# A feature-interaction tower on one core: the first level of a partial sum goes to an accumulating DMA, and a fourth product chunk is split

## The reference, cut to what matters

```python
e = stack([tbl_f[ids[:, f]] for f in range(39)])      # 1024 samples, 39 fields, 16 values each
x0 = xk = e
for W in (f0, f1, f2):                                # (39*39,128), (128*39,128), (128*39,128)
    z = einsum('bfd,bgd->bfgd', x0, xk).reshape(b, 39 * g, 16)
    xk = einsum('bpd,pm->bmd', z, W)
    outs.append(xk)
z = sum(concatenate(outs, axis=1), axis=-1)           # 1024 x 384
h = relu(concat(z, dense_ctx) @ W_top1 + b_top1)
h = relu(h @ W_top2 + b_top2)
y = h @ W_top3
```

## Time and profile before

| | |
|---|---|
| median of 3 runs (range) | 1400.6 us (1400.31 to 1401.37) |
| the profiled execution, and its span | 1401.89 us, 1400.1 us |
| PE busy | 1297.8 us (93%) |
| POOL busy, without the gaps between the gathers | 1040.9 us (74%) |
| DVE busy | 981.8 us (70%) |
| ACT busy | 773.4 us (55%) |
| mean granted PE clock | 0.999 of full |

### The profile page before, as it was taken

One profiled execution on the slowest core, in us unless ns is written; L12 is line 12 of the kernel. 1 busy time (PEld: TensorE's weight loads), 2 busy tenths in 40 slices (PEclk: granted clock), 3 DMA queues, 4 the chain that ended last, 5 costly groups with the idle time before them and its releaser, 6 DMA issues.

```text
span 1400.1 us, 25243 instructions
## 1 busy us (share of the span) xinstructions
PE 1297.8 (93%) x5629; PEld 982.7 (70%) x5629; DVE 981.8 (70%) x3243; ACT 773.4 (55%) x2449; POOL 1040.9 (74%) x921
## 2 busy tenths in 40 slices
PE   0199999999999999999999999999999999999999
PEld 0167677876787777777777777777778777777754
DVE  2078778586877878587876878688786878688720
ACT  2146666356646665467655566466664576456631
POOL 7668888686887878788886888788786866566530
PEclk9999999999999999999999999999999999999999
DMA  8122121110211121011211112111211101111000
GB/s 218 36 82 55 47 59 53 37 43 24 59 54 51 46 59 53 5 53 46 60 53 51 46 33 58 28 53 46 60 52 52 46 12 55 45 51 45 1 1 0
DMA packets 72379, 67.51 MB, mean 48 GB/s; under 512 B 32140, under 2 KB 44402, under 8 KB 72260
## 3 DMA queue, kind: packets, MB, share of 16 engines
q1 hardware_dynamic: 59556, 62.38, 15.0%
q0 software_dynamic: 9984, 2.58, 1.9%
q10 hardware_dynamic: 2720, 1.48, 0.4%
HBM read 10.15 MB, written 0.00 MB: 7 GB/s over the span
## 4 chain that ended last, share of the span: by engine, by line
PE 65%; DVE 15%; issue 10%; POOL 5%; ACT 2%; DMA 1%; DVEq 1%; SPq 0%; ACTq 0%; POOLq 0%
PE ps L456 13%; PE ps L460 13%; PE ps L457 13%; PE ps L435 13%; DVE terms L809 10%; PE ps L480 5%; DVE prods L781 4%; POOL x_in L328 3%; PE ps L470 3%; PE ps L545 2%; ACT terms L664 2%; PE ps L404 2%; POOL terms L351 2%; PE ps L555 1%; DVEq L808 1%
## 5 line engine op out<-in xcount | busy, mean ns | idle before, releaser
L809 DVE SCALAR_TENSOR_TENSOR terms<-ps,x_scal,terms 128x128 f32<-128x128 f32 x2944 | 814.8, 344 | 294.2 <-PE ps L460 182.6
L664 ACT ACTIVATE terms<-ps,x_scal 128x128 f32<-128x128 f32 x2048 | 586.1, 375 | 388.9 <-PE ps L460 359.8
L351 POOL TENSOR_TENSOR terms<-terms 128x1024 f32<-128x1024 f32 (+2 forms) x384 | 565.6, 1473 | 173.7 <-DVE terms L809 152.9
L456 PE MATMUL ps<-w_high,x_high 128*128 128x512 f32 (+1 forms) x1280 | 581.6, 454 | 3.8 <-ACT terms L664 1.7
L460 PE MATMUL ps<-w_high,x_low 128*128 128x512 f32 (+1 forms) x1280 | 498.7, 390 | 1.1 <-ACT x_rows L607 1.1
L457 PE MATMUL ps<-w_low,x_high 128*128 128x512 f32 (+1 forms) x1280 | 498.3, 389 | 0.0
L328 POOL DMA_INDIRECT x_in<-in_tbl,ids_now x312 | 299.8, 961 | 97.7 <-issue 86.1
L456 PEld LDWEIGHTS ps<-w_high,x_high 128*128 128x128 f32 x1280 | 240.9, 188 | 97.1 <-DVE terms L809 21.7
L457 PEld LDWEIGHTS ps<-w_low,x_high 128*128 128x128 f32 x1280 | 241.6, 189 | 73.5 <-issue 29.8
L460 PEld LDWEIGHTS ps<-w_high,x_low 128*128 128x128 f32 x1280 | 240.9, 188 | 54.5 <-ACT x_rows L607 2.0
L435 PE MATMUL ps<-prods,w 117*128 117x512 f32 x262 | 135.3, 602 | 5.0 <-DVE prods L781 5.0
(11 more groups left out here) (49 smaller groups left out, 525.7 us busy)
## 6 DMA issues: line engine op xcount, KB each, us to landing
prods<-x_cols SPq DMA_DIRECT2D x192, 234.0 KB
x_first<-x_cols SPq DMA_DIRECT2D x96, 78.0 KB
x_in<-in_tbl,ids_now POOLq DMA_INDIRECT x312
x_diag<-x_scal SPq DMA_DIRECT2D x256, 9.8 KB
s<-in_f SPq DMA_DIRECT2D x3, 832.0 KB, 13.3
wt<-in_W_top ACTq DMA_DIRECT2D x1, 768.0 KB, 8.1
wt<-in_W_top ACTq DMA_DIRECT2D x1, 512.0 KB, 9.3
terms<-in_w_pair SPq DMA_DIRECT2D x1, 409.5 KB
```

The source lines that it names most:

```text
L351: nc.gpsimd.tensor_tensor(t[:, 0:n], t[:, 0:n], t[:, n:2 * n], ALU.add).then_inc(s_tree, 1)
L456: nc.tensor.matmul(y, x1_high[:, par, at:at + P], high, start=True, stop=False)
L664: op = nc.scalar.activation(terms[:, u % 2, FB * ACT_BANKS.index(q) + i, :], ps[:, (BANKS * u + q) % RING, i * G:(i + 1) * G], ACT.Copy, s ...
L809: nc.vector.scalar_tensor_tensor(out=acc, in0=y, scalar=x0, in1=acc, op0=ALU.mult, op1=ALU.add).then_inc(s_mac, 1)
```

## The change

1. The tree's widest level goes. In its place POOL adds one pair of slots (128x128), then issues a DMA from its own queue which adds the seven upper slots onto the seven lower ones inside SBUF (128 rows of 896 values, 448 KB). A renumbering of the slots (`SLOTS`) puts DVE's two chains at slots 7 and 15, so that those are the pair that POOL adds itself; ACT's 14 others are the DMA's. POOL then waits for both and goes on with the levels of 4 and 2.
2. The step's two or three gathers are issued between that DMA and the wait for it, and no longer after the step's sum.
3. A fourth chunk of products, number 3, is split as the three others are: one more rounded copy at ACT, one more subtraction at POOL, three passes at PE for one float32 product.
4. PE takes the chunks in the order 4, 5, 6, 0, 1, 2, 3.

```diff
-SPLIT = (0, 1, 2)
+SPLIT = (0, 1, 2, 3)
-CIN1_ORDER = (0, 1, 3, 4, 5, 6, 2)
+CIN1_ORDER = (4, 5, 6, 0, 1, 2, 3)
-HIGHS = ((0, 2), (0, 4), (0, 7))
-POOL_LOWS = {0: (0, 1), 1: (2,)}
+HIGHS = ((0, 2), (0, 4), (0, 7), (0, 9))
+POOL_LOWS = {0: (0, 1), 1: (2, 3)}
-TREE = (8, 4, 2)
+TREE = (4, 2)
+HALF = TERMS // 2
+SLOTS = (HALF - 1, TERMS - 1) + tuple(i for i in range(TERMS) if i % HALF != HALF - 1)
...
                 pool.wait_ge(s_ya, bt * (STEPS * NA) + NA * (u + 1) + CREDIT_A)
                 pool.wait_ge(s_mac, bt * (STEPS * MACS) + MACS * (u + 1) + CREDIT_MAC)
+                nc.gpsimd.tensor_tensor(t[:, HALF - 1], t[:, HALF - 1], t[:, TERMS - 1], ALU.add).then_inc(s_pair, 1)
+                pool.dma_start(out=t[:, 0:HALF - 1], in_=t[:, HALF:TERMS - 1], accum_op=ALU.add).then_inc(s_acc, 16)
+                for f in fetch:
+                    gather(f)
+                pool.wait_ge(s_pair, bt * STEPS + u + 1)
+                pool.wait_ge(s_acc, bt * (16 * STEPS) + 16 * (u + 1))
                 for i, n in enumerate(TREE):
...
-                add_up(bt, wanted)
-                for n in range(STEPS - 1):
-                    for f in share(0, n, STEPS - 1):
-                        gather(f)
-                    add_up(bt, wanted + 1 + n)
+                for n in range(STEPS):
+                    add_up(bt, wanted + n, fetch=share(0, n, STEPS - 1) if n < STEPS - 1 else ())
...
-                        terms[:, u % 2, FB * ACT_BANKS.index(q) + i, :],
+                        terms[:, u % 2, SLOTS[FB * ACT_BANKS.index(q) + i], :],
...
-                    acc = terms[:, u % 2, n % CHAINS, :]
+                    acc = terms[:, u % 2, SLOTS[n % CHAINS], :]
```

More of the change, by code:

```diff
@@ L189, in cin_tower @@
         s_tree = sem("partial_adds")
+        s_pair = sem("chains_paired")
+        s_acc = sem("upper_half_accumulated")
         s_x2 = sem("x2_ready")
@@ L336, in prologue, with add_up @@
                     gather(f)
-            def add_up(bt, u, front=True):
+            def add_up(bt, u, front=True, fetch=()):
                 gf = bt * GROUPS + u // TILES + 1
+                t = terms[:, u % 2]
                 if front:
@@ L343, in add_up @@
                         split_low(pool, gf, i)
-                t = terms[:, u % 2]
                 pool.wait_ge(s_ya, bt * (STEPS * NA) + NA * (u + 1) + CREDIT_A)
                 pool.wait_ge(s_mac, bt * (STEPS * MACS) + MACS * (u + 1) + CREDIT_MAC)
+                nc.gpsimd.tensor_tensor(t[:, HALF - 1], t[:, HALF - 1], t[:, TERMS - 1], ALU.add).then_inc(s_pair, 1)
[4 more added lines that the diff above has]
+                pool.wait_ge(s_acc, bt * (16 * STEPS) + 16 * (u + 1))
                 for i, n in enumerate(TREE):
@@ L369, in _ @@
             for u in range(wanted):
-                if u < wanted - 1:
-                    for f in share(ahead, u, wanted - 1):
-                        gather(f)
-                add_up(0, u)
+                add_up(0, u, fetch=share(ahead, u, wanted - 1) if u < wanted - 1 else ())
             with pool.Fori(0, NBATCH - 2) as bt:
```

## The result

The changed kernel takes 1449.8 us (median, 1443.1 to 1451.2), the one before beside it 1401.0 (1400.3 to 1402.2). The ratio is 1.034 [1.031, 1.037]: 49 us slower, where the forecast was 1395 and its range ended at 1424. The profiled execution took 1449.2 us, with a span of 1447.1.

A forecast was written before the change was run, and what follows sets the result against it. PE and DVE were taken to bound the kernel in turns, with POOL nearly full but keeping up. From 1401.9 us, less 5.3 (split) and 2 (order), plus 1.5 (burst), came 1396.1, timed 1394.8, said as 1395; range 1391 to 1424.

The forecast's parts named there:

- SP's burst of product DMAs comes at tile 3's fifth bank and meets the DMAs of tiles 2 and 3; I add 1.5 us for that over the program.: Term for SP's product loads sharing the DMA engines with the new DMA: 1.5 us added over the program.
- just in time: Tile 3's step on POOL, 8.1 us with three gathers at x = 4.3, was to end exactly when due.
- The landing x: Time from the start of POOL's sum to the accumulating DMA's landing: taken as 4.3 to 4.7 us.
- The doubled data of the bound, x = 5.7: Upper case for the DMA's landing: reading both operands through the same engines doubles the data, 5.7 us.
- A: The forecast: the DMA is hidden under POOL's gathers; 1395 us, 1391 to 1398 for x from 4.3 to 4.7; chance 0.42.
- B: POOL's sum comes back late at x = 4.8 to 5.0, DVE loses what PE gains; 1398 to 1404 us; chance 0.20.
- due times: When ACT needs each tile's x2 from POOL, two steps later; margins a few tenths, tiles 0 and 1 2 us more.
- rival C: POOL becomes the bound at x2 of tiles 2 and 3, by x = 5.4 or a 1.3 us issue; 1418 to 1439; chance 0.38.
- POOL keeps up, and nothing waits for it for long: Reading of the kernel before: POOL needs 36.6 us of a group of 36.9.
- Half of its sign: Sign: PE's wait for products 2 us or more, and ACT waiting for x2 at tiles 0 and 1 in most groups.
- PE's saving and the order: At PE, the fourth split saves 0.17 us in 31 groups, 5.3 us, counted in full; the new chunk order saves 2.
- The stall of descriptor writing: Rule against the change: POOL's DMA issues stretch beside DVE's two-port adds, with rival C's result; 0.03 of its chance.

The follow-up runs named there:

- e3: Changed kernel with SP's product DMAs moving an eighth of their columns from the second group on; 1415.4 us, ratio 1.010.
- e6: Changed kernel without the DMA in tile 3, where POOL does the wide add itself and gathers behind the sum; 1404.7 us, ratio 1.004.
- e4: Changed kernel with the accumulating DMA made a plain copy, the lower seven slots left out of the sum; 1405.8 us, ratio 1.003.
- e7: Kernel before, no DMA, with the gathers moved inside POOL's sum, between the wide add and the levels of 4 and 2; 1413.1 us, ratio 1.009.
- e12: Kernel before with POOL's wide add taking only 64 of each slot's 128 columns; 1393.8 us, ratio 0.995.
- e11: Kernel before with the fourth split, the new chunk order and POOL's wide add on 64 of 128 columns; 1387.5 us, ratio 0.990.
- e5: Kernel before with three splits and only the chunk order changed, to 3, 4, 5, 6, 0, 1, 2; 1399.0 us, ratio 0.9984.
- e1: Kernel before with the fourth split and the new chunk order, without the DMA; 1400.8 us, ratio 0.9994.
- e9: Changed kernel with the gathers behind the sum, so that nothing covers the DMA; 1649.9 us, ratio 1.177.

## Why the prediction was wrong

- **The step that failed** is "SP's burst of product DMAs comes at tile 3's fifth bank and meets the DMAs of tiles 2 and 3; I add 1.5 us for that over the program." The place was right, the price was not: with a smaller burst 34 us come back (e3), with tile 3 as before 45 (e6). The average share of the batch, 0.17, stood for the moment of the transfer, at which the engines are full. And the term was added as time of its own, when by the steps ahead of it tile 3 ended "just in time": 1.2 us in its mean (6.49 over 5.27), and up to 4 in single steps, had almost no slack to go into.
- **The landing x.** Taken 4.3 to 4.7, measured 4.7 to 4.8 from the start of the sum where nothing is in the way (1351.22 less 1346.88 and 0.40 for the pair's add). The issue is 0.94 us, as taken. The doubled data of the bound, x = 5.7, turned out true of the engines' time (2.5 us against 1.3 in e4) but not of a lone landing. By its x alone the kernel lies between A and B, whose sums end at 1398 and 1404; B names no burst and does not reach the measured time either.
- **Behind three gathers** the tree starts 5.25 to 5.3 us behind the sum's start (forecast 5.4), and the rest of the step takes 2.6 (forecast 2.7). These terms held. So did the wait for the DMA, short behind two gathers (0.78 us at 478.00), outside the burst.
- **The gathers' latency ahead of `x2`** was weighed only by its due times, and by them tiles 0 to 2 were in time. e7 prices it at 12 us with no DMA at all. The due times came from one group of one batch and had margins of tenths; over the program ACT waits for `x2` in 68 steps of 128. The forecast's own sentence for rival C, "3 us of latency where 2.5 were spare", was the better reading.
- **"POOL keeps up, and nothing waits for it for long"** was already not so in the kernel before: with half of the widest level left out it is 7.4 us faster (e12). The forecast counted none of this.
- **Rival C** named the mechanism, POOL's sum as the bound with ACT waiting for `x2`, and its chance was 0.38. Its price was sized by an average step of 8.1 to 8.4 us, at 1418 to 1439. Half of its sign came: ACT waits for `x2` in 15 of 32 tiles 0 and 20 of 32 tiles 1, but PE's wait for products stayed at 39.7/31 = 1.3 us. Neither of the two conditions that it gave, x = 5.4 or an issue of 1.3 us, came true; the burst made the step longer instead. The measured average is (5.08 + 5.13 + 5.27 + 6.49)/4 + 2.6 = 8.1, and by that C would say 1418. The 30 us more are probably in the spread between the steps, as a late `x2` stops ACT, PE and DVE (the three waits at 541.49 to 542.76) and a short step later need not give that back. No run shows this apart, and the size stays open. The clock is a small part, about 1447 x (0.999 - 0.996) = 4 us (last section).
- **PE's saving and the order** were right in size: forecast 5.3 + 2, measured 6.3 where POOL is relieved (e11 against e12), and 2.2 for the order alone (e5). That the saving "counts in full" was not: with POOL as it was nothing of it is clear of the noise (e1). A chunk at the place (2,5) is 0.69 us from start to start, as forecast:

```profile
477.38 0.39 PE L439 MATMUL ps<-prods_high,w_high 117*128 117x512 f32 x1
...
478.07 0.35 PE L460 MATMUL ps<-w_high,x_high 128*128 128x384 f32 x1
```

- **What the Trainium skill gave.** The estimate of 3.1 us for the landing, by the Trainium skill's "DMA: Bandwidth & Descriptors" (Anatomy of one DMA), is near the plain copy's 2.9 us; the accumulation took 4.3. That the add reduces two streams, as the Trainium skill has it on the same page (SDMA does more than copy), fits with the doubled engine time. The stall of descriptor writing that the Trainium skill describes in "SBUF — State Buffer" (Who interferes with whom) does not show: the issues of the new DMA beside a busy DVE average 0.94 us, and the 33 of 128 that meet almost no work of DVE's 0.93. Whether DVE's adds run in a two-port mode no run here tells, so this is no test of the rule.

```profile
L353 POOL DMA_DIRECT2D terms<-terms x128 | 119.7, 935 | 1.2 <-issue 1.1
```

## What to carry to other kernels

Work that moves from an engine to a DMA takes its price from the moment of the transfer: list what else is in flight there, above all bursts on other queues, and take the share of that window and not of a batch. Where a chain is in time by tenths, don't add a delay as microseconds of its own; ask what stands still when it is late, and how often. A cover ahead of a result that others wait for is itself latency: cover a DMA with work that the result already had to wait for (here the subtractions, which stood ahead of the sum before), and leave out the places where the due time or the traffic is tight.

## What the runs showed of the hardware

- An accumulating DMA of 448 KB within SBUF takes the 16 engines 2.5 us where a copy takes 1.3, lands 4.3 us behind the start of its issue against 2.9, and its issue holds POOL for 0.94 us on average against 0.58 (e4).
- A DMA that meets a burst from another queue is stretched: beside SP's loads the DMA that lands in 4.3 us alone took until 8.4 us behind its issue (530.38 to 538.77), at a DMA share of 1.03. The plain copy, 2.9 us alone, took 6.0 in a tile 3 of e4.
- PE's granted clock can fall behind a stall. Windows of the changed kernel (the clock is the third number from the end), behind the 2.84 us in which PE stood still until 542.69:

```profile
543.00:544.00 1.00, 1.00 (x6) 0.63 (x4) 1.00 (x5) 1.00 (x6) 1.00 (x2) 0.89 0.00 0
544.00:545.00 1.00, 1.00 (x3) 0.87 (x3) 1.00 (x4) 1.00 (x5) 1.00 (x2) 0.50 0.02 8
546.00:547.00 1.00, 0.84 (x1) 0.50 (x2) 1.00 (x5) 0.00 (x0) 0.70 (x2) 0.50 1.15 209
547.00:548.00 1.00, 1.00 (x4) 0.53 (x3) 1.00 (x5) 0.00 (x0) 0.77 (x1) 0.91 1.09 188
```

0.50 is 1.2 GHz, the lower of the two levels. PE's own timeline in that stretch:

```profile
543.25 0.39 PE L464 MATMUL ps<-w_high,x_low 128*128 128x512 f32 x1
...
545.11 0.63 PE L464 MATMUL ps<-w_high,x_low 128*128 128x512 f32 x1
546.16 1.62 PE L439 MATMUL ps<-prods,w 117*128 117x512 f32 x2 [0.43 <-DVE prods L785]
...
548.10 0.39 PE L464 MATMUL ps<-w_high,x_low 128*128 128x512 f32 x1
```

A pass goes from 0.39 us to 0.63 and back, and a float32 chunk takes 1.62 where it took 1.02. The clock fell in the same way behind a stall of 2.05 us that ended at 748.44 (0.50 from 749 to 751), but stayed at 1.00 behind one of 2.56 us that ended at 210.45, so the length of the stall alone does not tell. The mean clock of the changed kernel is 0.996, that of e9 0.959. So a late engine can cost a little twice.
